# All source indices kept in SBUF and a gather ring of 32 slots instead of 16, in a one-core graph transformer layer

## The reference

```
h   = layer_norm(x) @ W.T
msg = h[row] * norm[:, None]                 # one row of h for every edge
out = segment_sum(msg, col, num_segments=n)  # summed by destination
x   = x + relu(out + b)
```

```
y   = einsum('teh,ehd->ted', gelu(einsum('td,edh->teh', xf, W1) + b1), W2) + b2
out = einsum('ted,te->td', y, mask)
```

## Time and profile before

| | |
|---|---|
| median of three runs | 4768.15 us |
| span of the profiled execution | 6592.7 us |
| PE matmul busy in it | 4352.7 us (66%) |
| POOL busy | 3207.3 us (49%) |
| DVE busy | 2648.4 us (40%) |
| ACT busy | 1212.7 us (18%) |
| gathers (main and rest) | 3136 and 196 |
| mean granted TensorE clock | 0.81 of full speed |

### The profile page before, as it was taken

How to read it: one execution, slowest core, us unless ns; L and a number is a source line. 1 busy time by engine, 2 the same in 40 slices (tenths; PEclk the granted TensorE clock), 3 DMA queues, 4 the chain that set the end, 5 groups by cost and what they waited for, 6 DMA issues and landing times.

```text
span 6592.7 us, 100628 instructions
## 1 busy us (share of the span) xinstructions
PE 4352.7 (66%) x28316; PEld 3508.3 (53%) x28317; DVE 2648.4 (40%) x9845; ACT 1212.7 (18%) x3196; POOL 3207.3 (49%) x3354
## 2 busy tenths in 40 slices
PE   5855555555555555555557777777777777777778
PEld 4744444444444444444446656665666666665656
DVE  6643333333333343333334444443444444444444
ACT  1310000000000000000012222222322222222223
POOL 0035555555555555555545454545555555554552
PEclk8977777777777777777778888888888888888888
DMA  2032333323233233233232222222222222222221
GB/s 102 22 106 82 91 91 87 88 87 90 86 89 90 84 91 91 82 92 90 83 84 80 74 80 75 80 75 80 79 78 79 78 79 80 79 81 74 79 81 47
DMA packets 264728, 538.48 MB, mean 82 GB/s; under 512 B 64504, under 2 KB 157056, under 8 KB 264704
## 3 DMA queue, kind: packets, MB, share of 16 engines
q0 software_dynamic: 159936, 436.95, 23.5%
q1 hardware_dynamic: 104768, 101.25, 4.6%
HBM read 498.20 MB, written 39.71 MB: 82 GB/s over the span
## 4 chain that ended last, share of the span: by engine, by line
another core or an unknown queue 36%; PE 33%; issue 14%; DVE 7%; ACT 5%; DVEq 4%; SPq 1%; DMA 0%; POOL 0%; ACTq 0%; POOLq 0%
PE bank L1042 32%; ACT hT L549 3%; DVEq L231 2%; DVE ss L809 1%; PE bank L1064 1%; DVE hT_low L941 1%; ACT hT_high L552 1%; DVEq L236 1%; ACT L549 1%; ACT L532 1%; ACT hT L520 1%; DVE rstd L570 0%; DVE rstd L569 0%; DVE rstd L568 0%
## 5 line engine op out<-in xcount | busy, mean ns | idle before, releaser
L415 POOL DMA_INDIRECT gs<-h_d,idx_s x3136 | 3015.9, 962 | 3168.8 <-DVE idx_s L806 1808.7
L1042 PE MATMUL bank<-gs,ss 128*128 128x256 f32 x6272 | 1822.0, 440 | 121.5 <-issue 76.2
L1042 PEld LDWEIGHTS bank<-gs,ss 128*128 128x128 f32 x6272 | 1357.8, 225 | 371.1 <-issue 140.8
L1042 PE MATMUL bank<-nT_high,experts 128*128 128x128 f16 x6528 | 734.9, 234 | 225.1 <-issue 207.7
L809 DVE TENSOR_SCALAR ss<-iw,dst_f,ew 128x128 f32<-128x128 f32 x3152 | 881.9, 352 | 0.5 <-issue 0.5
L1042 PE MATMUL bank<-experts,hT_high 128*128 128x256 f16 x3264 | 680.7, 308 | 210.3 <-DVE hT_low L941 149.8
L941 DVE SCALAR_TENSOR_TENSOR hT_low<-hT,hT_high 128x512 f16<-128x512 f32 x408 | 282.7, 693 | 1257.3 <-ACT hT_high L552 1108.4
L549 ACT ACTIVATE hT<-bank,eb1c 128x128 f32<-128x128 f32 x1632 | 465.9, 368 | 1585.0 <-remote 1286.1
L1042 PEld LDWEIGHTS bank<-nT_high,experts 128*128 128x128 f16 x6528 | 570.0, 106 | 296.9 <-issue 278.8
L1042 PE MATMUL bank<-nT_low,experts 128*128 128x128 f16 x3264 | 648.4, 234 | 87.4 <-issue 87.1
L1042 PE MATMUL bank<-w,hT 128*128 128x256 f32 x392 | 177.1, 632 | 574.8 <-ACT hT L520 570.0
(11 more groups left out here) (235 smaller groups left out, 4194.7 us busy)
## 6 DMA issues: line engine op xcount, KB each, us to landing
gs<-h_d,idx_s POOLq DMA_INDIRECT x3136
hself<-h_d SPq DMA_DIRECT2D x100, 128.0 KB
ew_in<-in_eW SPq DMA_DIRECT2D x49, 168.0 KB
out<-u SPq DMA_DIRECT2D x51, 128.0 KB
u<-xn_d SPq DMA_DIRECT2D x50, 128.0 KB
h_d<-u SPq DMA_DIRECT2D x50, 128.0 KB
u<-x_d SPq DMA_DIRECT2D x50, 128.0 KB
u<-r_d SPq DMA_DIRECT2D x50, 128.0 KB
```

Of the source, the lines that this page charges most:

```text
L415: pool.indirect_dma_start(gs[:, slot, :], None, table[:, :], bass.IndirectOffsetOnAxis(ap=idx_s[:, slot:slot + 1], axis=0)).then_inc(s[f"m ...
L1042: return pe.matmul(out_ap, lhsT, rhs, start=first, stop=last, **kw)
```

## The change

The indices of all chunks of all blocks are copied once, in the first stage, to a resident list `idx_all` (one DVE copy of 32 columns for each block, behind the degree work). The copies to `idx_s` disappear. `gs` gets 32 slots, one for each chunk of a window; `ss` stays at 16. POOL's loops over windows are written out, and each gather waits only until TensorE has used the chunk that had its slot 32 gathers before (in layer 1 also once per block until that block is listed). The rest gathers of window w move: they stand now behind the next window's first 20 gathers in layer 1, and behind its first 24 in layer 2, instead of behind its first 4. The room for the larger ring comes from buffers of layer 2 that are now laid over `w1`, which layer 2 does not use.

```diff
-SLOTS = 16
-EARLY = 1
+SLOTS = STATIC
+S_SLOTS = 16
+EARLY = (20, 24)
...
-        idx_s = sb("idx_s", [P, SLOTS], I32); idx_r = sb("idx_r", [P, RU], I32)
+        idx_all = sb("idx_all", [P, W, STATIC], I32); idx_r = sb("idx_r", [P, RU], I32)
         gs = sb("gs", [P, SLOTS, D]); gr = sb("gr", [P, RU, D])
-        ss = sb("ss", [P, SLOTS, P]); sr = sb("sr", [P, RU, P])
+        ss = sb("ss", [P, S_SLOTS, P]); sr = sb("sr", [P, RU, P])
...
-                def groups(w, some):
-                    for n in range(some.start * U, some.stop * U):
-                        slot = n % SLOTS
-                        if n % U == 0:
-                            pool.wait_ge(s["idx_set"], layer * W * STATIC + w * STATIC + n + U)
-                            pool.sem_inc(s["pool_gate"], 1)
+                def chunks(w, some):
+                    for n in some:
+                        g = (layer * W + w) * STATIC + n
+                        if layer == 0 and n == 0:
+                            pool.wait_ge(s["idx_listed"], w + 1)
+                        if g >= SLOTS:
+                            pool.wait_ge(s["main_used"], g - SLOTS + 1 + S_SLOTS)
                         pool.indirect_dma_start(
-                            gs[:, slot, :], None, table[:, :],
-                            bass.IndirectOffsetOnAxis(ap=idx_s[:, slot:slot + 1], axis=0)).then_inc(s[f"main_in{slot}"], 16)
+                            gs[:, n, :], None, table[:, :],
+                            bass.IndirectOffsetOnAxis(ap=idx_all[:, w, n:n + 1], axis=0)).then_inc(s[f"main_in{n}"], 16)
...
-                groups(0, range(0, EARLY))
-                with pool.Fori(0, W - 1) as w:
-                    groups(w, range(EARLY, PIECES))
-                    ranges = rest_table(pool, layer, w)
-                    groups(w + 1, range(0, EARLY))
-                    rest(*ranges)
-                groups(W - 1, range(EARLY, PIECES))
-                rest(*rest_table(pool, layer, W - 1))
+                chunks(0, range(EARLY[layer]))
+                for w in range(W):
+                    chunks(w, range(EARLY[layer], STATIC))
+                    if w < W - 1:
+                        chunks(w + 1, range(EARLY[layer]))
+                    rest(*rest_table(pool, layer, w))
...
+                dve.tensor_copy(idx_all[:, bass.ds(t, 1), :].rearrange("p a c -> p (a c)"),
+                                src_row[:, bass.ds(lo, STATIC)]).then_inc(s["idx_listed"], 1)
...
                 dve.wait_ge(s["main_used"], v + k * U + U)
-                slot = k * U % SLOTS
-                dve.tensor_copy(idx_s[:, slot:slot + U], src_row[:, bass.ds(first + k * U, U)]).then_inc(s["idx_set"], U)
+                slot = k * U % S_SLOTS
...
-                    pe.wait_ge(s[f"main_in{n % SLOTS}"], 16 * (turn * (STATIC // SLOTS) + n // SLOTS + 1))
-                    mm(acc, ss[:, n % SLOTS, :], gs[:, n % SLOTS, :], fresh and n == 0, True,
+                    pe.wait_ge(s[f"main_in{n}"], 16 * (turn + 1))
+                    mm(acc, ss[:, n % S_SLOTS, :], gs[:, n, :], fresh and n == 0, True,
```

More of the change, by code:

```diff
@@ L162, in gps_kernel @@
         vx = sb("vx", [P, KB, P + 1])
-        hT = [sb(f"hT{i}", [P, HBLK, P]) for i in range(2)]
-        hT_part = [[sb(f"hT_{n}{i}", [P, HBLK, P], F16) for n in ("high", "low")] for i in range(2)]
-        nT_part = [sb(f"nT_{n}", [P, KB, P], F16) for n in ("high", "low")]
+        hT0 = sb("hT0", [P, HBLK, P])
         st = sb("st", [P, 12]); mv = sb("mv", [P, 4]); rstd = sb("rstd", [P, 8])
@@ L191, in gps_kernel @@
         touch = [flat_ss[:, i * W * RB:(i + 1) * W * RB].rearrange("p (w b) -> p w b", w=W) for i in range(3)]
-        assert 3 * W * RB <= SLOTS * P
+        assert 3 * W * RB <= S_SLOTS * P
         dst_i = dst_f[:, :].bitcast(I32)
@@ L208, in take @@
                 return piece if dt == F32 else piece.bitcast(dt)
+        ffn_room = Carve(w1[:, :, :].rearrange("p k n -> p (k n)"), 0, 2 * KB * HID)
+        hT = [hT0, ffn_room.take(HBLK * P).rearrange("p (j n) -> p j n", j=HBLK)]
+        hT_part = [[ffn_room.take(HBLK * P, F16).rearrange("p (j n) -> p j n", j=HBLK) for _ in range(2)] for _ in range(2)]
+        nT_part = [ffn_room.take(KB * P, F16).rearrange("p (k n) -> p k n", k=KB) for _ in range(2)]
         tail = Carve(experts, W * D, W * EW_STEP)
@@ L1031, in _ @@
         def _(pe):
-            pe.sem_inc(s["main_used"], SLOTS)
+            pe.sem_inc(s["main_used"], S_SLOTS)
             pe.sem_inc(s["rest_used"], REST_FROM + RU)
```

## The result

The changed kernel takes 4790.51 us (median of 4 runs, 4789.48 to 4791.76). The kernel before, run beside it, takes 4770.16 us (4 runs, 4761.47 to 4774.55). The ratio is 1.0045 with a 95% interval of 1.0031 to 1.006: 20.4 us slower, about half of the 38 us forecast (4806), and inside the forecast's own range of 4783 to 4840.

A forecast was written before the change was run, and what follows sets the result against it. POOL's pace of 1.25 us a gather was taken as the bound: 4768 + 5 (list) + 18 + 25 (fill, layers 1 and 2) - 10 (contention) = 4806 us, +0.8%. Range 4690 to 4845; the forecast's own 4783 to 4840.

The forecast's parts named there:

- POOL's pace is the bound: Both layers: POOL needs at least 34 x 1.25 = 42.5 us a window, and the timed kernel already runs at that pace.
- Fill, 18 and 25 us: Ends of layers 1 and 2: TensorE trails POOL further because rest gathers come later, costing 18 and 25 us, once each.
- Index list, 5 us: First stage: 49 added index copies cost 0 to 10 us, depending on what TensorE's degree products hide; 5 taken.
- Gathers at 1.25 us in both layers: Layers 1 and 2: 1666 gathers each, at 0.95 us plus a 0.30 us gap, without POOL waiting.
- Copies removed, 0 us: Both layers: DVE's 788 copies to idx_s lie beside POOL's work; removal gains 0, at most 122.6 us.
- contention given back, 10 us: Gathers in both layers: DVE work lengthens them by 41 us in all; removing copies returns 0 to 41, 10 taken.
- 122.6 us of room: Whole kernel before: median 4768.15 less 4645.6 us with POOL never waiting, left for waits or anything else.
- rival 1: Both layers: the 122.6 us are waits for index copies; 4694 us if all go, 4755 if half; chance 0.27.
- Waits per gather and the written-out code, 0 us: POOL's loops: wait and loop code stay hidden behind the gather's 0.95 us of descriptor work; price 0, otherwise up to 245.
- Rival 4: POOL's loops: stalls on written-out code or single waits in every window, up to 4806 + 245 us; chance 0.05.
- Rival 3: POOL's gathers: faster pace when nothing is recorded, 1.10 us each, giving about 4500 us; chance 0.08 together with the port rule.
- what is special to the profiled execution: Layer 1 window: three silent stretches, 25.8 us together, where the next engine idles though its producer is done.

The follow-up runs named there:

- after again: The changed kernel, unchanged, run where the kernel before takes 6605.6 us instead of about 4770: 5926.5 us, ratio 0.8966.

## Why the prediction was right, and where it was off

*POOL's pace is the bound: shown.* The step is 1.25 us in after's trace as in the earlier trace rows, with all but three gaps of 0.30 us, and the two layers together are 4254.3 us of gathers out of 4788.7.

*Fill, 18 and 25 us: right in mechanism and size, wrong in where it would show.* Waits of 17.0 and 29.7 us stand in the changed kernel's own trace. Putting the rest gathers 20 later can't cost more than 20 steps of 1.25 us, so of the 29.7 us only 25.0 are due to the move. With the early place POOL would have come to the last rest gathers 35.3 us behind those of window 47; in layer 1 their indices were there by then (POOL went on 32.5 us behind them), in layer 2 not (40.1 us). That makes a fill of 17.0 and 25.0 us and a wait of 4.7 us in layer 2 that before would have had too, an estimate from after's trace. The fill is confirmed as a difference of 29.9 us (38.6 in the layers of the two traces) where only the place was changed at POOL's pace. I had written that POOL would stand longer between the layers than 20.9 us and that the time behind the last gather would be longer than 64.9. They are 17.9 and 64.8. The wait stands ahead of the last rest gathers instead. My working let these go out at POOL's pace; but their indices are not in the resident list, and DVE copies them late in the same window, so POOL meets TensorE's lag two gathers before the end of the layer and not behind it.

*Index list, 5 us: low.* The first stage is 405.0 us against 394.8, 10.2 us: my upper bound, 49 copies with their dispatch at 0.2 us each (the trace has 0.17 us for one), as if TensorE's degree products hid none of them. (405.4 us under the stretched conditions, in after again, so this stage hardly depends on them.)

*Gathers at 1.25 us in both layers: low in layer 2.* Gathers and gaps take 2095.9 us in layer 1, 13.4 over 2082.5, and 2158.4 us in layer 2, 75.9 over. The durations of the gathers add up to 1588.7 us in layer 1 and 1651.2 in layer 2. Above 946 ns each, layer 2 has 75.2 us of lengthening, and 64.6 of it is in the 522 gathers that overlap a run of line 945. Two pairs from the timeline, each a gather and an instruction of DVE. In the first line 945 starts behind the gather, in the second ahead of it:

```profile
3608.47 0.95 POOL L420 DMA_INDIRECT gs<-h_d,idx_all  x1 [0.30 <-issue]
3608.73 0.69 DVE L945 SCALAR_TENSOR_TENSOR w<-hT,w 128x512 f16<-128x512 f32 x1 [1.65 <-ACT w L555]
...
3613.21 0.69 DVE L945 SCALAR_TENSOR_TENSOR w<-w 128x512 f16<-128x512 f32 x1 [1.82 <-ACT w L555]
...
3613.50 1.22 POOL L420 DMA_INDIRECT gs<-h_d,idx_all  x1 [0.30 <-issue]
```

The others follow this pattern: 257 gathers that start while line 945 is running take 0.24 us longer on average, 61.4 us together, and 231 gathers into which line 945 starts 0.2 us or more behind their start take 0.0 us longer. So the two contend, and it is the gather's start that is held up. The source in layer 2 is mostly not the index copies that the change removes; it is an operation of DVE that the change leaves alone. The 41 us of lengthening that I read in the earlier trace rows came from stretched conditions, and there the 417 gathers beside which an index copy ran carry 5 us of it. No run took line 945 away.

The Trainium skill, page "SBUF — State Buffer", section "Who interferes with whom", says that a DVE instruction with two inputs in SBUF contends with a GpSimd instruction that reads SBUF, and not with one that only writes it. The trace agrees: line 945 has two such inputs, a gather takes its indices from `idx_all` in SBUF, and the gathers beside line 945 carry 64.6 of the 75.2 us.

*Copies removed, 0 us, and contention given back, 10 us: too little.* This is the term that was most mis-sized. With after's pace put into before's other stages, before would be 394.8 + 2095.9 + 20.9 + 2158.4 + 64.9 = 4734.9 us, and 4739.6 with its own wait of 4.7. It is 4770.2, so some 30 us of before were none of these, and most of the 122.6 us of room was pace (13.4 + 75.9). Fill (42.0), first stage (10.2) and the shorter stretches between the layers and behind the last gather (-3.1) add up to +49.1; measured is +20.4, so about 29 us came back. What of them was waiting for the copies, which is rival 1 at a quarter of its size, and what their contention with POOL (5 us in the trace of before), stays open: no trace of before exists under the timed conditions, and none of the twelve runs fell into them. That the result lies in the forecast's range owes something to luck: the list cost 5 us more than forecast, and against it stand 19 us more given back and 3 us between the layers and behind them.

*Waits per gather and the written-out code, 0 us: right.* The steps are unchanged, and no gap is longer than 0.3 us that the fill and the turn of the layers don't explain. Rival 4 is out. *Rival 3* (a faster pace when nothing is recorded) is out too: the trace's 4788.7 us and the timed 4790.51 agree, with steps of 1.25 us. *The ring of 32, 0 us*: in the timed conditions no run took it alone; POOL's waits in after are all explained without it. In stretched conditions it gains nothing at the early place and loses 1398 us against the ring of 16.

*The reading of the profile of before: right for the wrong reason.* That the timed execution runs at POOL's pace followed from the count of needs (42.5 us against 36.2 and 41 to 43), and held. But "what is special to the profiled execution" was not: before takes 6602 to 6695 us in timed runs of other chips. Had the change been timed there, the forecast of +0.8% would have met -10.3%, for in those conditions it is rival 1 that decides: POOL's 1894.2 us of waits for copies vanish, and the kernel with the list alone, at the old ring and place, has the whole gain. The forecast rested on the stated median, and that is all that made it safe.

*A better version.* In stretched conditions it is the list with the ring of 16 and rests behind 12, 5661.3 us, 14.3% below before. In the timed conditions the trace of after suggests the list with the rests at their early place: 4790.5 less the 42.0 us of fill is about 4748, an estimate from after's two waits. It wasn't measured there, and in stretched conditions that very kernel is the slowest of all.

## What to carry to other kernels

Before costing a change, ask whether the profile and the timed runs show the same machine: if the span is far from the median, work out what each engine needs for a window from durations and steps, and settle the bound by that and not by the list of waits. In that list, read times and longest beside the total: 711 us in 2335 waits of 0.3 is no wait, and 47.3 in 2 is the finding. Moving work later in a pipeline whose pace is set by its first engine costs at most the distance once per phase, in the last wait of each phase (25.0 of 29.7 us in layer 2), and it buys nothing if that engine never waited.

## What the runs showed of the hardware

- The same program took 4770 us in one place and 6602 to 6695 us on the chips of the experiments, with identical steps of POOL (0.95 + 0.30 us). The difference lies in stretches like those above, in which all engines but POOL pause or issue slowly. In the one shown they stop some six gathers into a row and go on 2 to 3 us behind its end; in after again only half of the long `remote` waits end within 4 us of the beginning of a pause. A step of 1.6 us all but ends them (`remote` waits of VectorE and ScalarE: 25 us with the rests late, 109 us with the rests behind 4, against 3732 us in after again); with the memset of 0.30 us and a step of 1.42 us they still come (3267 us). Why some chips or conditions have them is open.
- A main gather of 128 rows of 1 KB costs 0.95 us and a gap of 0.30 us. A memset of one byte in each partition (0.12 us) fits whole into that gap and leaves the step at 1.25 us; one of 0.30 us makes it 1.42 us, and one of 0.45 us 1.57 us, both with a wait for the memset before.
- A gather that starts while VectorE runs line 945 (two inputs in SBUF, 0.69 us) takes 0.24 us longer on average; if line 945 starts 0.2 us or more into the gather, nothing is added.
- From the issue of a gather to its landing it takes 2.8 us (median).
